# Layer norm of two quads from a host-transposed x, and a host-transposed dense weight, in a pre-norm attention layer

## The chip, the cores and the metric

The kernel runs on one core of one Trainium2 chip. The metric is the device time of one execution in microseconds (us): the median of three runs.

## What is computed

x is [8, 256, 512] float32, 2048 rows of 512. Cut to what matters, the reference is:

```
x = x + attn(layernorm(x)) ; x = x + ffn(layernorm(x))
attn: qkv = h @ w_qkv; 32 query heads, 8 key/value heads of 128; causal, bias -slope * sqrt(distance);
      out = softmax(q k^T * scale + bias) v, then out @ w_o
ffn:  dots = softmax(h @ centroids.T / 0.1); hits = dots > 0.01
      out = where(any_hit_of_row & any_hit_of_cluster[assignments], h @ weight.T + bias, 0)
```

weight is [512, 512] and centroids is [64, 512]; both are used transposed.

## The kernel before, in words

**Layout.** The 2048 rows are 4 quads of 512 (two batches each). Attention works in 32 units: unit u takes key/value head u // 4, with its 4 query heads, on quad u % 4. Float32 products go through TensorE as three passes over a high and a low part (`three_pass`), so each operand is held as `..._hi` (a copy rounded by ACT) and `..._lo` (the rest, from DVE or POOL).

**One unit on PE** is `body`: six projections (k, four q, v: `project(u, 0)` to `project(u, 5)`), with the probabilities of the unit before applied to v between them (`apply_v(u, c)`, chunks c = 0 to 5), four output projections (`project_out(u, 0)` to `(u, 3)`) and the eight score blocks `scores(u, 0)` to `(u, 7)`. Chunks 0 to 3 are applied at steps i = 2 to 5 of the projection loop, chunk 4 behind `project_out(u, 0)`, chunk 5 behind `scores(u, 1)`.

**Way of a chunk.** DVE turns 32x32 blocks of the probabilities (`turn`, L926), SP sends the tile to DRAM (`turn_out`, L399) and reads it back permuted (`turn_in`, L404), ACT makes the high part (`pT_hi_part`, L666), POOL the low part (`pT_lo_part`, L523), PE uses both. v goes the same way (`turn_v`, L418 and L430, then `v_hi_part` on ACT, L692). Every engine works in the order in which its program is written, and SP waits for each semaphore in turn: a DMA that is not ready holds back those written behind it. All of SP's DMAs go through one queue.

**Scores.** DVE adds the bias and takes the row maximum (`add_bias(u, i)`, L956 and L963), ACT takes the exponential (`exps`, L677) and scales by the reciprocal row sum (`normalise`, L686), DVE turns. `scores(u, i)` waits until `add_bias` has been done up to i - 2, since there are two banks.

**Layer norm before projection.** The norm of quad L (L = 1, 2, 3) is made inside unit L - 1, that of quad 0 ahead. DVE takes statistics (`ln_stats_of`, L847; `ln_var`, L859), ACT the root (`ln_root`, L642), DVE a refinement (`ln_scale`, L871 to L874) and the four normalised tiles (`ln_apply`, L886); PE transposes each in four 128x128 pieces (`ln_transpose`, L1270) at steps 4 and 5; ACT and DVE copy the result as `xnT` high and low (`ln_hi` L646, `ln_lo` L891). After attention the same is done for the second norm, numbered 4 to 7.

**Feed-forward weights.** In unit 29 SP loads weight, centroids, assignments and bias (L438 to L443). Ahead of unit 30 PE transposes weight and centroids in 16 + 4 pieces (L1500, L1504), ACT and DVE copy them (L795, L1153). Units 30 and 31 also carry the second norm of quads 0 and 1 and their clusters and dense products.

**Loops.** Units 0 to 2 are written out, 3 to 29 are a hardware loop on PE, ACT and DVE; SP loops over the chunks of units 0 to 28. The order of the second half of the projection loop on PE is this:

```
if lag <= i < CHUNKS - 2 + lag:
    apply_v(u, i - lag)
if L is not None and i >= 4:
    ln_transpose(L, 2 * i - 8)
    ln_transpose(L, 2 * i - 7)
```

## Time and profile before

| | |
|---|---|
| median of three runs | 1261.96 us (1261.77 to 1262.03) |
| the profiled execution's own time | 1263.28 us |
| its span, first to last instruction | 1261.6 us |
| granted TensorE clock, mean | 0.999 of full speed |
| PE busy | 1244.7 us, 99% of the span |
| DVE, ACT, POOL busy | 762.5, 752.5, 516.0 us |
| PE in the chain that ended last | 90% |

The profile is of one execution. "Unit 1" lies at about 38 to 82 us of its span, unit 2 at 82 to 120, unit 29 at 1059 to 1095, unit 30 at 1098 to 1150. Start times are counted from the first instruction. Lengths of matmuls overlap: the next one starts before the end of the last that is shown, so durations on PE are read from start to start.

### The profile page before, as it was taken

How to read it: one execution, taken by the hardware profiler on the slowest of the kernel's cores; microseconds unless marked ns; L12 is line 12 of the kernel's file. 1: busy time of each engine (PE TensorE's matmuls, PEld its weight loads, DVE VectorE, ACT ScalarE, POOL GpSimd, SP SyncE). 2: the span in 40 equal slices, each digit the busy share in tenths (PEclk: the TensorE clock that was granted, in tenths of full speed). 3: DMA queues.
4: the chain of work that ended last, by engine and by line, in shares of the span. 5: the costliest groups of instructions: out<-in, count | busy, mean ns of one | idle time of the engine just before them, and what ended most of it. 6: DMA issues, size and time to landing. Idle time of an engine off the chain costs nothing.

```text
span 1261.6 us, 21930 instructions
## 1 busy us (share of the span) xinstructions
PE 1244.7 (99%) x6188; PEld 1051.4 (83%) x6188; DVE 762.5 (60%) x2156; ACT 752.5 (60%) x2154; POOL 516.0 (41%) x476
## 2 busy tenths in 40 slices
PE   8899999999999999999999999999999999999998
PEld 7688888888888888888888888888888888888786
DVE  7777555555555555555555555655555556677677
ACT  3776555666655556666556566665566666656543
POOL 6322636227342555226442364327362364223313
PEclk9999999999999999999999999999999999999999
DMA  6422334324342344333333344323243343422103
GB/s 225 134 92 79 122 116 158 116 100 150 99 133 84 121 136 129 129 103 130 108 121 104 123 143 124 125 91 127 98 149 116 108 150 115 135 67 92 61 16 134
DMA packets 162377, 147.14 MB, mean 117 GB/s; under 512 B 10032, under 2 KB 123696, under 8 KB 162352
## 3 DMA queue, kind: packets, MB, share of 16 engines
q1 hardware_dynamic: 156528, 128.48, 30.8%
q0 software_dynamic: 5824, 18.36, 4.9%
q8 instruction: 12, 0.20, 0.1%
q14 instruction: 13, 0.11, 0.0%
HBM read 84.67 MB, written 62.13 MB: 116 GB/s over the span
## 4 chain that ended last, share of the span: by engine, by line
PE 90%; DVE 5%; ACT 2%; issue 1%; DMA 1%; POOL 0%; DVEq 0%; SPq 0%; ACTq 0%
PE ps L1250 83%; PE ps L1351 3%; PE ps L1352 1%; PE ps L1270 1%; ACT prob L677 1%; DVE stats L847 1%; ACT prob L686 1%; DVE ring_whole L926 1%; DVE qT_lo L901 1%; DVE rs L872 0%; PE ps L1280 0%; DVE prob L886 0%; DMA acc<-in_L_attn_hidden_states 0%; DVE prob L963 0%; PE ps L1382 0%
## 5 line engine op out<-in xcount | busy, mean ns | idle before, releaser
L1250 PE MATMUL ps<-xnT,wqkv_hi 128*128 (+1 forms) x1552 | 480.1, 390 | 1.3 <-DVE kT L898 1.3
L523 POOL TENSOR_TENSOR ring<-ring_whole,pT_hi 128x512 fp32r<-128x512 f32 x189 | 244.0, 1291 | 483.3 <-ACT pT_hi L666 483.0
L1250 PEld LDWEIGHTS ps<-xnT,wqkv_hi 128*128 128x128 f32 x1552 | 288.6, 188 | 61.5 <-DVE kT L898 1.7
L677 ACT ACTIVATE prob<-prob,negmax 128x128 f32<-128x128 f32 (+1 forms) x512 | 226.8, 445 | 178.3 <-DVE negmax L963 177.4
L1250 PE MATMUL ps<-xnT,wqkv_lo 128*128 (+1 forms) x776 | 302.1, 389 | 0.0
L686 ACT ACTIVATE prob<-prob,rinv 128x128 f32<-128x128 f32 (+1 forms) x512 | 190.3, 445 | 62.5 <-DVE rinv L971 62.3
L1250 PE MATMUL ps<-wo_hi,oT_hi 128*128 128x512 f32 x512 | 201.9, 394 | 0.0
L1250 PE MATMUL ps<-wo_lo,oT_hi 128*128 128x512 f32 x512 | 199.8, 390 | 0.0
L1250 PE MATMUL ps<-wo_hi,oT_lo 128*128 128x512 f32 x512 | 199.3, 389 | 0.0
L1250 PEld LDWEIGHTS ps<-xnT,wqkv_lo 128*128 128x128 f32 x776 | 145.7, 188 | 30.5
L943 DVE TENSOR_TENSOR acc<-ps,acc 128x512 f32 (+1 forms) x128 | 88.4, 691 | 127.6 <-PE ps L1250 127.4
L901 DVE SCALAR_TENSOR_TENSOR qT_lo<-ps,qT_hi 128x512 fp32r<-128x512 f32 x128 | 87.2, 681 | 118.3 <-ACT qT_hi L655 118.3
L926 DVE STREAM_TRANSPOSE ring_whole<-prob 128x512 f32<-128x512 f32 x189 | 130.0, 701 | 45.0 <-ACT prob L686 45.0
L655 ACT ACTIVATE qT_hi<-ps 128x512 fp32r<-128x512 f32 x128 | 76.2, 595 | 106.3 <-PE ps L1250 105.8
L666 ACT ACTIVATE pT_hi<-ring_whole 128x512 fp32r<-128x512 f32 x189 | 118.4, 627 | 22.7 <-DMA ring_whole<-turned 19.8
L670 ACT ACTIVATE oT_hi<-ps 128x512 fp32r<-128x512 f32 x128 | 76.0, 594 | 74.5 <-PE ps L1250 69.5
L1250 PEld LDWEIGHTS ps<-wo_hi,oT_lo 128*128 128x128 f32 x512 | 96.1, 188 | 20.4
L1250 PEld LDWEIGHTS ps<-wo_hi,oT_hi 128*128 128x128 f32 x512 | 96.3, 188 | 18.2
L1250 PEld LDWEIGHTS ps<-wo_lo,oT_hi 128*128 128x128 f32 x512 | 96.4, 188 | 17.8
L937 DVE TENSOR_TENSOR oT_lo<-ps,oT_hi 128x512 fp32r<-128x512 f32 x128 | 88.3, 690 | 32.3 <-ACT oT_hi L670 32.3
L963 DVE CUSTOM_DVE_ANT_0 prob<-ps,bias 128x256 f32<-128x256 f32 x256 | 94.3, 421 | 10.7 <-DVE ring_whole L926 8.5
L677 ACT ACTIVATION_READ_ACCUMULATOR prob<-prob,negmax 128x1 f32 x512 | 96.0, 187 | 0.0
(139 smaller groups left out, 1731.9 us busy)
## 6 DMA issues: line engine op xcount, KB each, us to landing
turned<-ring_whole SPq DMA_DIRECT2D x189, 256.0 KB, 2.1
ring_whole<-turned SPq DMA_DIRECT2D x189, 256.0 KB, 3.0
turned_v<-vT SPq DMA_DIRECT2D x32, 256.0 KB, 2.0
vT<-turned_v SPq DMA_DIRECT2D x31, 256.0 KB, 2.7
raw<-in_L_attn_w_qkv POOLq DMA_DIRECT2D x28, 256.0 KB, 3.2
raw<-in_L_attn_w_o POOLq DMA_DIRECT2D x28, 256.0 KB, 3.3
raw<-in_L_attn_w_qkv POOLq DMA_DIRECT2D x28, 128.0 KB, 3.1
acc<-in_L_attn_hidden_states SPq DMA_DIRECT2D x3, 1024.0 KB, 7.7
```

The lines of the kernel that those rows point to most:

```text
L523: pool.tensor_tensor(ring_slot(c), whole_slot(c), pT_hi[:, c % 2, :].bitcast(F32), ALU.subtract).then_inc(pT_lo_done, 1)
L655: ins = act.activation(qT_hi[:, i - 1, :], src, ACT.Copy, scale=SCALE)
L666: act.activation(pT_hi[:, c % 2, :], source, ACT.Copy).then_inc(pT_hi_done, 1)
L670: act.activation(oT_view(u, oT_hi, k), pv_view(u, k), ACT.Copy).then_inc(oT_hi_done, 1)
L677: ins = act.activation(s, s, ACT.Exp, bias=negmax[:, n:n + 1], scale=-1.0, accum_out=rowsum[:, n:n + 1])
L686: ins = act.activation(s, s, ACT.Copy, scale=rinv[:, n:n + 1])
L901: ins = dve.scalar_tensor_tensor(qT_lo[:, i - 1, :], src, SCALE, qT_hi[:, i - 1, :].bitcast(F32), ALU.mult, ALU.subtract)
L926: dve.transpose(whole_slot(c).rearrange("p (j h c) -> p h j c", h=HPG, c=BLK), source.rearrange("p h (j c) -> p h j c", c=BLK)).then_inc(p ...
L937: dve.tensor_tensor(oT_view(u, oT_lo, k), pv_view(u, k), oT_view(u, oT_hi, k).bitcast(F32), ALU.subtract).then_inc(oT_lo_done, 1)
L943: dve.tensor_tensor(acc[:, at], ps[:, out_bank(u, k), :], acc[:, at], ALU.add).then_inc(added, 1)
L963: ins = dve.tensor_tensor_reduce(out=s, in0=ps[:, score_bank(u, i), bank_col:bank_col + (qt + 1) * P], in1=bias[:, h, :] if qt else s, sca ...
L1250: ins = pe.matmul(dst, l, r, start=start and m == 0, stop=stop and m == n - 1)
```

## The change

**x by rows.** The host passes x also transposed (`in_x_t`, [512, 2048]). For quads 2 and 3, SP loads 1 MB of it (`load_xt`) straight into the place where `xnT` low of the quad will stand (`xw` is the same memory as `xnT`). DVE computes mean and scale as before, but all four statistics at step 0, and copies the means beside the scales (`ln_rows`). SP writes these 128 x 8 numbers to DRAM in token order (`send_stats`), element by element, and reads the two rows of 512 back, broadcast to all 128 partitions (`spread_stats`). POOL subtracts and multiplies chunks 0 to 2 (`centre`, `scale_xt`), DVE chunk 3 (`last_chunk`), ACT makes the high parts (`xt_hi`), POOL the low parts (`xt_lo`). The transposes, `ln_apply`, `ln_hi` and `ln_lo` of these two quads are gone. Quads 0 and 1, and the second norm, are as before.

**Dense weight and centroids.** The host passes both transposed. The 20 PE transposes are gone. The weight is loaded (1 MB) into quad 1's place of `xnT`, so SP waits until unit 29's projections are done; ACT makes the high part in unit 30 (`w_hi`, steps 2 and 3), POOL the low part between its chunks.

**Loops.** PE's unit 3 and SP's units 0 to 2 are written out.

```
+        xw = sb("xw", [P, QUADS, 2, TPQ, UT], F32, below)
-        wT_hi, wT_lo = xnT[:, 1, 0], xnT[:, 1, 1]
+        wT_hi, wT_lo, wT_raw = xnT[:, 1, 0], xnT[:, 1, 1], xw[:, 1, 1]
-        w_raw = sb("w_raw", [P, NC, HID], F32, ffn)
-        c_raw = sb("c_raw", [CLUSTERS, HID], F32, ffn)
+        c_raw = sb("c_raw", [P, NC, CLUSTERS], F32, ffn)
+        def by_rows(L):
+            return L is not None and 2 <= L < QUADS
+        def nth(L):
+            return L if L < 2 else L - 2
...
 @@ SP
+            def load_xt(L):
+                sp.dma_start(xw[:, L, 1], x_t[:, L * UT:(L + 1) * UT].rearrange("(c p) t -> p c t", p=P)).then_inc(xt_loaded, 16)
+            def send_stats(L):
+                n = L - 2
+                sp.wait_ge(stat_ready, n + 1)
+                sp.dma_start(stat_rows[n].rearrange("s (j p) -> p s j", p=P), rs[:, 4:6, :], allow_slow_non_contiguous=True).then_inc(stat_out, 16)
+            def spread_stats(L):
+                n = L - 2
+                sp.wait_ge(stat_out, 16 * (n + 1))
+                sp.dma_start(xw[:, L, 0, 2:4, :], stat_rows[n].rearrange("(a s) t -> a s t", a=1)
+                             .broadcast_to([P, 2, UT])).then_inc(stat_in, 16)
+            def turn_half_and_stats(v, L):
+                turn_out(v, 3)
+                turn_in(v, 3)
+                turn_out(v, 4)
+                send_stats(L)
+                turn_out(v, 5)
+                turn_in(v, 4)
+                spread_stats(L)
+                turn_in(v, 5)
-            with sp.Fori(0, UNITS - 3) as v:
+            turn_v(0)
+            load_xt(2)
+            turn_half(0, 0)
+            turn_half_and_stats(0, 2)
+            turn_v(1)
+            load_xt(3)
+            turn_half(1, 0)
+            turn_half_and_stats(1, 3)
+            turn_v(2)
+            turn_half(2, 0)
+            turn_half(2, 1)
+            with sp.Fori(QUADS - 1, UNITS - 3) as v:
...
-            sp.dma_start(w_raw[:], w_ffn.rearrange("(t p) d -> p t d", p=P)).then_inc(wc_loaded, 16)
-            sp.dma_start(c_raw[:], cents).then_inc(wc_loaded, 16)
+            sp.dma_start(c_raw[:], cents_t.rearrange("(c p) n -> p c n", p=P)).then_inc(c_loaded, 16)
+            sp.wait_ge(qkv_mm, PROJ_OUTS * (UNITS - QUADS + 2))
+            sp.dma_start(wT_raw, w_ffn_t.rearrange("(c p) n -> p c n", p=P)).then_inc(w_loaded, 16)
...
 @@ POOL
+            def centre(L, c):
+                if c == 0:
+                    pool.wait_ge(xt_loaded, 16 * (L - 1))
+                    pool.wait_ge(stat_in, 16 * (L - 1))
+                pool.tensor_tensor(xw[:, L, 1, c, :], xw[:, L, 1, c, :], xw[:, L, 0, 2, :], ALU.subtract).then_inc(xt_centred, 1)
+            def scale_xt(L, c):
+                pool.wait_ge(xt_centred, (NC - 1) * (L - 2) + c + 1)
+                pool.tensor_tensor(xw[:, L, 1, c, :], xw[:, L, 1, c, :], xw[:, L, 0, 3, :], ALU.mult).then_inc(xt_scaled, 1)
+            def xt_lo(L, c):
+                pool.wait_ge(xt_hi_done, NC * (L - 2) + c + 1)
+                pool.tensor_tensor(xnT[:, L, 1, c, :], xw[:, L, 1, c, :], xnT[:, L, 0, c, :].bitcast(F32),
+                                   ALU.subtract).then_inc(xt_lo_done, 1)
             for u in range(1, QUADS - 1):
-                plain_body(u)
+                for c in range(CHUNKS):
+                    pT_lo_part(u, c)
+                for c in range(NC - 1):
+                    centre(u + 1, c)
+                for c in range(NC - 1):
+                    scale_xt(u + 1, c)
+                for c in range(NC):
+                    xt_lo(u + 1, c)
+                v_lo_part(u)
...
+            u = UNITS - 2
+            for c in range(CHUNKS):
+                pT_lo_part(u, c)
+                for n in {3: (0,), 4: (1,), 5: (2, 3)}.get(c, ()):
+                    pool.wait_ge(wT_hi_done, n + 1)
+                    pool.tensor_tensor(wT_lo[:, n, :], wT_raw[:, n, :], wT_hi[:, n, :].bitcast(F32),
+                                       ALU.subtract).then_inc(wT_lo_done, 1)
+            v_lo_part(u)
...
 @@ ACT
+                    if p == 0 and i in (2, 3):
+                        w_hi(2 * i - 4)
+                        w_hi(2 * i - 3)
-                        if i == 2:
+                        if i == (1 if by_rows(L) else 2):
                             ln_root(L)
-                        if i >= 4:
+                        if i >= 4 and not by_rows(L):
...
                         elif i < 4:
+                            if by_rows(L) and i == 3:
+                                xt_hi(L, 2)
+                                xt_hi(L, 3)
                             normalise(u, i - 2)
+                            if by_rows(L) and i == 2:
+                                xt_hi(L, 0)
+                                xt_hi(L, 1)
...
 @@ DVE
+            def ln_rows(L):
+                dve.tensor_copy(rs[:, 4, :], meanvar[:, :, 0]).then_inc(stat_ready, 1)
+            def last_chunk(L):
+                dve.wait_ge(xt_loaded, 16 * (L - 1))
+                dve.wait_ge(stat_in, 16 * (L - 1))
+                x = xw[:, L, 1, NC - 1, :]
+                dve.tensor_tensor(x, x, xw[:, L, 0, 2, :], ALU.subtract).then_inc(last_centred, 1)
+                dve.wait_ge(last_centred, L - 1)
+                dve.tensor_tensor(x, x, xw[:, L, 0, 3, :], ALU.mult).then_inc(last_scaled, 1)
...
+                    if by_rows(L):
+                        if i == 0:
+                            for j in range(TPQ):
+                                ln_stats_of(L, source, j)
+                            ln_var(L)
+                        elif i == 1:
+                            ln_scale(L)
+                            ln_rows(L)
...
                 if attn:
                     add_out(u, 1)
+                if by_rows(L):
+                    last_chunk(L)
...
 @@ PE
                     if i == 0:
                         pe.wait_ge(raw_split, (u >> 2) * (2 * NC) + c + 1)
+                        if isinstance(u, int) and by_rows(u):
+                            pe.wait_ge(xt_lo_done, NC * (u - 2) + c + 1)
...
-                    if L is not None and i >= 4:
+                    if L is not None and i >= 4 and not by_rows(L):
...
-                    if L is not None and attn:
-                        pe.wait_ge(ln_lo_done, L * TPQ + TPQ)
+                    if L is not None and attn and not by_rows(L):
+                        pe.wait_ge(ln_lo_done, nth(L) * TPQ + TPQ)
...
                     pe.wait_ge(oT_lo_done, u * QTILES + QTILES)
+                    pe.wait_ge(wT_lo_done, NC)
                     dense(p, 0)
...
-            with pe.Fori(QUADS - 1, UNITS - 2) as u:
+            body(QUADS - 1, True, True)
+            with pe.Fori(QUADS, UNITS - 2) as u:
                 body(u, True, True)
-            pe.wait_ge(wc_loaded, 32)
-            pe.wait_ge(oT_lo_done, QTILES * (UNITS - 2))
-            for t in range(NC):
-                for c in range(NC):
-                    ins = pe.transpose(ps[:, WT_BANKS[t], c * P:(c + 1) * P], w_raw[:, t, c * P:(c + 1) * P], ident[:])
-                ins.then_inc(wT_mm, 1)
...
```

**SP, unit 1.** The queue of unit 1 handles the chunks of unit 0. Before (one turn of the loop, from chunk 3 on):

```order
L399 DMA turned<-ring_whole 128x512
L404 DMA ring_whole<-turned 128x4x128
L398 REGISTER_ALU
L399 DMA turned<-ring_whole 128x512
L398 REGISTER_ALU
L399 DMA turned<-ring_whole 128x512
L404 DMA ring_whole<-turned 128x4x128 x2
```

Now, from the reading back of v on:

```order
L451 DMA vT<-turned_v 128x4x128
L456 DMA xw<-in_x_t 128x4x512
L420 DMA turned<-ring_whole 128x512
L425 DMA ring_whole<-turned 128x4x128
...
L420 DMA turned<-ring_whole 128x512
L462 DMA stat_rows<-rs 128x8x1
L420 DMA turned<-ring_whole 128x512
L425 DMA ring_whole<-turned 128x4x128
L468 DMA xw<-stat_rows 128x1024
L425 DMA ring_whole<-turned 128x4x128
```

The 1 MB load stands ahead of chunk 0's way out; the statistics go out ahead of chunk 5's way out, and come back ahead of chunk 5's way in.

**DVE, unit 1,** from the turning of chunk 3. Before:

```order
L926 STREAM_TRANSPOSE ring_whole<-prob 128x4x4x32
L847 BN_STATS stats<-acc 128x6 x2
L901 SCALAR_TENSOR_TENSOR qT_lo<-ps,qT_hi 128x512
L926 STREAM_TRANSPOSE ring_whole<-prob 128x4x4x32
L847 BN_STATS stats<-acc 128x6 x2
L856 BN_AGGR meanvar<-stats 128x2 x4
L859 TENSOR_SCALAR rs<-meanvar 128x4
```

Now:

```order
L1048 STREAM_TRANSPOSE ring_whole<-prob 128x4x4x32
L956 BN_STATS stats<-acc 128x6 x4
L965 BN_AGGR meanvar<-stats 128x2 x4
L968 TENSOR_SCALAR rs<-meanvar 128x4
L1023 SCALAR_TENSOR_TENSOR qT_lo<-ps,qT_hi 128x512
L1048 STREAM_TRANSPOSE ring_whole<-prob 128x4x4x32
L980 RECIPROCAL rs<-rs 128x4
L981 TENSOR_TENSOR rs<-rs 128x4
L982 SCALAR_TENSOR_TENSOR rs<-rs 128x4
L983 SCALAR_TENSOR_TENSOR rs<-rs 128x4
L988 COPY rs<-meanvar 128x4
```

All statistics stand ahead of `proj_lo(1, 1)` and of the turning of chunk 4, and the refinement follows at once.

**SP, unit 29.** Before:

```order
L438 DMA w_raw<-in_L_ffn_weight 128x4x512
L439 DMA c_raw<-in_L_ffn_centroids 64x512
L440 DMA assigned<-in_L_ffn_assignments 64x512
L443 DMA bias_bc<-in_L_ffn_bias 128x512
L418 DMA turned_v<-vT 128x512
```

Now:

```order
L497 DMA c_raw<-in_L_ffn_centroids 128x4x64
L499 DMA xw<-in_L_ffn_weight 128x4x512
L500 DMA assigned<-in_L_ffn_assignments 64x512
L503 DMA bias_bc<-in_L_ffn_bias 128x512
L439 DMA turned_v<-vT 128x512
```

The order is nearly the same, but the weight's load waits for the sixth projection of unit 29, the one that also releases `turned_v`.

## Rows read from the trace of the kernel before

**Rows 1.** The page: busy us, share and count of each engine.

```profile
PE 1244.7 (99%) x6188; PEld 1051.4 (83%) x6188; DVE 762.5 (60%) x2156; ACT 752.5 (60%) x2154; POOL 516.0 (41%) x476
```

**Rows 2.** Timeline of PE, unit 1: start us, length us, line, operation, [idle before].

```profile
57.92 0.39 PE L1250 MATMUL ps<-pT_hi,v_lo 128*128 128x512 f32 x1
...
60.49 0.71 PE L1250 MATMUL ps<-xnT,wqkv_hi 128*128 128x512 f32 x2
...
64.02 1.04 PE L1270 MATMUL ps<-ident,prob 128*128 128x128 f32 x8
64.81 0.48 PE L1250 MATMUL ps<-wo_hi,oT_hi 128*128 128x512 f32 x1
...
69.18 0.45 PE L1250 MATMUL ps<-pT_hi,v_hi 128*128 128x512 f32 x1
...
77.24 0.34 PE L1351 MATMUL ps<-kT,qT_hi 128*128 128x256 f32 x1
```

**Rows 3.** Timeline of PE, unit 2.

```profile
97.60 0.60 PE L1270 MATMUL ps<-ident,prob 128*128 128x128 f32 x4
...
98.91 0.71 PE L1250 MATMUL ps<-xnT,wqkv_hi 128*128 128x512 f32 x2
```

**Rows 4.** Timeline of PE, end of unit 29, the weight's turn, unit 30.

```profile
1094.73 0.40 PE L1250 MATMUL ps<-kT,qT_hi 128*128 128x256 f32 x2
...
1095.45 1.91 PE L1500 MATMUL ps<-ident,w_raw 128*128 128x128 f32 x16
...
1097.99 0.73 PE L1250 MATMUL ps<-xnT,wqkv_hi 128*128 128x512 f32 x2
```

**Rows 5.** Timeline of SP's DMA issues, chunks of unit 0 (during unit 1).

```profile
36.97 0.37 SPq L430 DMA_DIRECT2D vT<-turned_v  x1
40.11 0.33 SPq L399 DMA_DIRECT2D turned<-ring_whole  x1
42.12 0.37 SPq L404 DMA_DIRECT2D ring_whole<-turned  x1
...
57.58 2.13 SPq L404 DMA_DIRECT2D ring_whole<-turned  x2
```

**Rows 6.** Timeline of SP's DMA issues, the feed-forward loads in unit 29.

```profile
1073.92 0.37 SPq L438 DMA_DIRECT2D w_raw<-in_L_ffn_weight  x1
...
1078.70 0.34 SPq L418 DMA_DIRECT2D turned_v<-vT  x1
1084.60 0.38 SPq L430 DMA_DIRECT2D vT<-turned_v  x1
```

**Rows 7.** DMA issues on the page (count, KB each, us to landing), and L385's landings.

```profile
ring_whole<-turned SPq DMA_DIRECT2D x189, 256.0 KB, 3.0
...
vT<-turned_v SPq DMA_DIRECT2D x1, 128.0 KB, 2.3
...
DMA to landing us min/median/max: 5.3/7.7/9.9
```

**Rows 8.** Timeline of ACT, units 1 and 29.

```profile
46.16 0.51 ACT L677 ACTIVATE prob<-prob,negmax 128x256 f32<-128x256 f32 x1 [0.31 <-DVE negmax L963]
...
1087.42 0.63 ACT L692 ACTIVATE v_hi<-vT 128x512 fp32r<-128x512 f32 x1 [1.69 <-DMA vT<-turned_v]
```

**Rows 9.** Timelines of DVE and POOL near 14 us, and the page's L523.

```profile
13.98 1.72 DVE L1133 TENSOR_TENSOR wqkv_lo<-acc,wqkv_hi 128x768 fp32r<-128x768 f32 x1
14.83 2.57 POOL L480 TENSOR_TENSOR wqkv_lo<-acc,wqkv_hi 128x768 fp32r<-128x768 f32 x1
L523 POOL TENSOR_TENSOR ring<-ring_whole,pT_hi 128x512 fp32r<-128x512 f32 x189 | 244.0, 1291 | 483.3 <-ACT pT_hi L666 483.0
```

**Rows 10.** Timeline of DVE, units 1, 29 and 30.

```profile
75.13 0.17 DVE L971 RECIPROCAL rinv<-rowsum 128x4 f32<-128x4 f32 x1
...
1094.04 0.29 DVE L963 CUSTOM_DVE_ANT_0 prob<-ps,prob 128x128 f32<-128x128 f32 x1
...
1114.08 0.99 DVE L886 TENSOR_SCALAR prob<-acc,meanvar,rs 128x512 f32<-128x512 f32 x2
```

More of the change, by code:

```diff
@@ L42, with build @@
 QTILES = 4
-def build(nc, x_in, w_qkv, w_o, w_ffn, b_ffn, cents, assign, out):
+def build(nc, x_in, x_t, w_qkv, w_o, w_ffn_t, b_ffn, cents_t, assign, out):
     ctx = ExitStack()
@@ L68, in build @@
         query_sel = sb("query_sel", [P, 2, TPQ], F32)
+        below = ExitStack()
+        xw = sb("xw", [P, QUADS, 2, TPQ, UT], F32, below)
+        below.close()
         att = ExitStack()
@@ L122, in build @@
         ffn.close()
+        stat_rows = [nc.dram_tensor(f"stat_rows{n}", [2, UT], F32, kind="Internal").ap() for n in range(2)]
         turned = nc.dram_tensor("turned", [CHUNKS, P, 512], F32, kind="Internal").ap()
@@ L188, in build @@
         ln_lo_done = sem("ln_lo_done")
+        xt_loaded = sem("xt_loaded")
+        stat_ready = sem("stat_ready")
+        stat_out = sem("stat_out")
+        stat_in = sem("stat_in")
+        xt_centred = sem("xt_centred")
+        xt_scaled = sem("xt_scaled")
+        last_centred = sem("last_centred")
+        last_scaled = sem("last_scaled")
+        xt_hi_done = sem("xt_hi_done")
+        xt_lo_done = sem("xt_lo_done")
         ffn_step = sem("ffn_step")
@@ L644, in ln_hi, with xt_hi @@
             def ln_hi(L, j, quad):
-                act.wait_ge(ln_mm, L * TPQ + j + 1)
+                act.wait_ge(ln_mm, nth(L) * TPQ + j + 1)
                 act.activation(ln_part(quad, 0, j), ps[:, ln_bank(L, j), :].rearrange("p (c t) -> p c t", c=NC),
                                ACT.Copy).then_inc(ln_hi_done, 1)
+            def xt_hi(L, c):
+                act.wait_ge(xt_scaled, (NC - 1) * (L - 2) + (c + 1 if c < 2 else NC - 1))
+                if c >= 2:
+                    act.wait_ge(last_scaled, L - 1)
+                act.activation(xnT[:, L, 0, c, :], xw[:, L, 1, c, :], ACT.Copy).then_inc(xt_hi_done, 1)
             def proj_hi(u, i):
@@ L725, in scaled_bias, with w_hi @@
                                    scale=selects(p)[:, j:j + 1]).then_inc(bias_scaled, 1)
+            def w_hi(c):
+                act.wait_ge(w_loaded, 16)
+                act.activation(wT_hi[:, c, :], wT_raw[:, c, :], ACT.Copy).then_inc(wT_hi_done, 1)
             def body(u, proj, attn, L=None, quad=None, p=None, lag=2):
@@ L881, in ln_apply @@
                     dve.wait_ge(p_turned, u * CHUNKS)
-                if not (isinstance(L, int) and L == 0):
-                    dve.wait_ge(ln_mm, L * TPQ - TPQ + j + 1)
-                    if j >= PROB_TILES and not (isinstance(L, int) and L >= 6):
-                        dve.wait_ge(ln_mm, L * TPQ + 1)
+                if L > 0:
+                    dve.wait_ge(ln_mm, nth(L) * TPQ - TPQ + j + 1)
+                    if j >= PROB_TILES and L < 6:
+                        dve.wait_ge(ln_mm, nth(L) * TPQ + 1)
                 dve.tensor_scalar(ln_tile(L, j), acc[:, rows(quad, j, 1)], meanvar[:, j, 0:1], rs[:, 5, j:j + 1],
```

60 lines of the change are left out of this document (26 added, 34 removed).

## The prediction

> **What bounds the kernel now.** I read the page first, for which engine fills the span: PE is busy 99% of it, DVE and ACT 60%, POOL 41% [rows 1]. So a change pays only by what it takes off PE's program or out of its waits, and costs whatever makes PE wait. Next came PE's timeline in the places that the change touches, where the reader should see from start to start how long the transposes hold PE [rows 2 to 4]; then SP's list of DMA issues there, for the order in the one queue and for the time at which the next issue shows the last landing [rows 5, 6], and the landing times [rows 7]; then ACT and DVE, for how much later each could have been without PE noticing [rows 8, 10]; last a place where DVE and POOL both work in SBUF [rows 9].
>
> **What goes off PE.** Unit 1: after the matmul at 57.92 the next would start one step, 0.23, later, at 58.15; the projection resumes at 60.49, so the first two groups of transposes hold PE 2.3 us, half of it waiting for DVE. The other two take 64.02 to 64.81, 0.8 [rows 2]. Unit 2: 97.60 to 98.91 is 1.3 [rows 3], and its second pair is the same work as unit 1's, 0.8. Weight and centroids: 1095.45 to 1097.99, 2.5 [rows 4]. Together 32 + 20 transposes, **7.7 us**, and there is no cover over them: it is all on the path.
>
> **What comes back.** Five things, each a wait that is not there before.
>
> *The load of x in unit 1.* SP issues it behind the reading back of v at 36.97, so at 37.4, and 2.7 us later chunk 0 goes out behind it, at 40.11, where it landed by 42.12 [rows 5]. The queue keeps its order: `turned_v`, issued at 1078.70 behind the 1.5 MB begun at 1073.92, landed at 1084.60, after 5.9 us instead of 2.0 [rows 6]. A load of 1 MB landed after 5.3 us at best, 7.7 in the middle [rows 7]; with the end of v ahead of it I take 6, so 43.4, and chunk 0 about 0.4 behind it, 43.8, which is 1.7 late. ACT takes chunk 0 in without idling, and idles 0.31 right behind it [rows 8]; ACT's exponentials and the k copy behind them are what PE waits for in unit 1. So 1.7 - 0.3 = **1.4** is lost. The ends: 0, if the engines serve both, and 3.2 with 7.7 for the load. In unit 2 the load is issued some 11 us before chunk 0, and costs nothing.
>
> *The statistics in the queue.* They are ready in unit 1 at about 56 to 57, as DVE does them in one go. No row shows a DMA of 1024 packets of 4 bytes. The nearest are 512 packets in 2.3 and 3.0 [rows 7], against 2.0 for 128 packets [rows 5]; 1024 make about 4, between 2.0 and 6. Then 512 KB are spread, and chunk 5's way in, issued at 59.3 before (the second of the two at 57.58 [rows 5]), goes out at about 60.9 behind them. It lands 3.0 [rows 7] plus some 1.7 for the 512 KB later, at 65.6; ACT adds 0.6 [rows 8], POOL 1.3 [rows 9]: 67.5. PE wants it at 69.18 [rows 2] less the 3.1 taken off in unit 1, plus the 1.4 that delay all engines alike, which cancel: 66.1 against 67.5. Since SP, POOL and ACT can start some of it sooner than my latest times, I take half, **0.7** (0 to 3). In unit 2 only 2.1 have gone off PE by then, so there is 1 us more room: 0.
>
> *The two operations on DVE* (`last_chunk`), one in each of units 1 and 2, fall into POOL's run of `centre` and `scale_xt`. Rows 9 show what that means: DVE's operation on 768 columns starts at 13.98 and ends at 15.70, 1.72 for what would need some 0.9 alone (1.5 x 0.6 for 512 columns, my estimate from the 0.5 of a tile with one input [rows 10]); POOL's, shown from 14.83, takes 2.57 where 768 columns need 1.5 x 1.29 = 1.94. They take turns in SBUF, whole instructions each. So DVE's two need 1.2 alone and up to 3.8; I take 2.9, half a POOL instruction ahead of the first and nearly a whole one ahead of the second. The cover: the bias of score block 3 was done at 75.13 [rows 10], and block 5, which waits for it, started at 77.24 [rows 2], 2.1 later. That leaves 0.8. Behind it ACT has `xt_hi`, four copies of about half a us [rows 8] between its exponentials, and the probabilities of half a unit pass it later; I add 0.3. Twice 1.1 is **2.2** (0 to 4).
>
> *The weight's load in unit 29.* It may start only after the sixth projection, at about 1077.9, 4.0 us later than before, at the very moment at which v is to go out. With assignments and bias it needs 7 to 8 us, so v is out at about 1087 instead of 1084.60 [rows 6]. ACT waited 1.69 for it already at 1087.42 [rows 8], so all of 2.4 delays ACT. Block 7 of the scores, at 1094.73 [rows 4], waits for a bias done at 1094.33 [rows 10]: 0.4 of cover, and I allow 1.0 for DVE's wait for PE between. It leaves **1.0** (0 to 2.5).
>
> *Unit 30.* POOL's four `wT_lo` of 1.29 stand between its chunks. DVE's `ln_apply`, at 1114.08, needs 0.5 for each tile [rows 10] and is of the kind that takes turns with POOL. PE is already waiting for it there, as in unit 2. **0.8** (0 to 1.3).
>
> At nothing I cost: the copies taken from ACT and DVE (60% busy, waiting for others at that place); ACT's `w_hi`, under a wait for PE in unit 30; the ten instructions of 1.29 on POOL per quad, 12.9 us, which follow chunk 5 at about 67 and end near 81, just before unit 2's projections at about 82 minus the gain want them (`v_lo(1)` is queued behind, and is wanted 5 us into unit 2). If that cover is gone, PE waits at `xt_lo_done`, up to 2 us. The loop's unrolling costs nothing: units 1 and 2 were written out already.
>
> **The sum.** 7.7 - 1.4 - 0.7 - 2.2 - 1.0 - 0.8 = 1.6 us gained. The profiled execution took 1263.28 in all, so 1261.7 for the changed kernel; the median shown lies 1.3 lower, at 1261.96, and so the forecast is 1260.4. A measurement of this kernel tells 0.2%, 2.5 us, from no change.
>
> **A page against the row.** Writing 1024 single elements to DRAM is what the row of 2.3 us [rows 7] bounds only from afar. The Trainium skill's "VectorE: DVE Perf Modes", section "The three transpose paths", says that a plain DMA with transposing strides is 19 times slower than the X-bar's 1309 ns for 128x128. By it 1024 elements would need an estimated 1.6 us over the fixed time, 3.6 in all where I take 4, and the sum would be 0.2 to 0.4 better; nothing here shows it.
>
> **Rivals.** *Most of it stays.* The five waits lie under slack that I count too small: DVE's two operations slip between POOL's (1.2 in place of 2.9, covered by the 2.1), chunk 5 is in time, DVE and POOL miss each other in unit 30. For it: ACT and DVE get four to eight instructions fewer just there. Against: rows 9. What is left is the load of x, 1.4, and half of the weight's, 0.5, with some 0.8 of small waits: 7.7 - 2.7 = 5.0, so 1257.0.
>
> *The small packets are slow, and it is slower than before.* If the statistics land after 8 us rather than 4, chunk 5 comes 4 later. PE waits 4.0 more in unit 1 and 3.0 in unit 2, where 1 us was left: 1.6 - 7.0 = -5.4, so 1267.4. It decides from about 6.2 us of landing on, where the gain becomes a loss of 2.5. For it: every chunk behind shares the queue. Against: halving the run from 512 to 256 bytes, at the same number of packets, made the landing shorter, 2.3 for 3.0 [rows 7]. The Trainium skill's "DMA: Bandwidth & Descriptors", section "Specifications", speaks for it: below 512 bytes the DMA does read-modify-write. No run here shows that for writes to DRAM.
>
> **How the numbers follow.** The forecast gets 0.52, most staying 0.36, slow packets 0.12. The forecast's own range is about 1258.5 to 1263.5; of its 0.52 I give 0.03 to faster by over 0.2% and 0.01 to slower. That makes faster 0.39, same 0.48, slower 0.13. The range for 8 in 10 reaches from 1256.0, just beyond the second case, to 1264.2, where the terms of unit 1 are at their upper ends, and leaves out the slow packets.
>
> **What would show it.** Right: 52 fewer matmuls on PE; in unit 1 ACT's first copy of a chunk waits for its DMA some 1.5 us; a wait of PE of about 0.7 ahead of chunk 5; waits of PE for DVE ahead of score blocks 4 to 7 in units 1 and 2, about 1 us each; DVE's `last_chunk` instructions over 1 us long; ACT waiting some 4 us for v in unit 29. From first projection to first projection, the sum says: unit 1 as long as before (3.1 - 1.4 - 0.7 - 1.1 = -0.1), unit 2 1.0 shorter (2.1 - 1.1), units 29 and 30 with the weight 0.7 shorter (2.5 - 1.0 - 0.8). Wrong: a landing of the statistics above 6 us; or blocks 4 to 7 without a wait, which would give the second rival.

## The result and the profile after

The changed kernel takes **1281.62 us** (median of 4 runs, 1280.77 to 1282.54), the kernel before 1261.87: the ratio is 1.0155, 95% interval 1.0143 to 1.0167, so 20 us slower. The prediction said 1260.4, within 1256.0 to 1264.2. It was wrong. The profiled execution took 1282.54, its span is 1280.9.

| from first projection to first projection, us | unit 1 | unit 2 | units 3 to 29 | from unit 30 on |
|---|---|---|---|---|
| before | 43.44 | 38.43 | 977.64 | 163.6 |
| after | 55.51 | 48.14 | 975.01 | 163.8 |
| difference | +12.07 | +9.71 | -2.63 | +0.2 |

The loss lies in units 1 and 2 alone. Everything else together gained 2.5. (The +0.2 from unit 30 on flatters the change: in the profiled execution of the kernel before, the granted clock of TensorE, PE's engine, was 0.50 for some 3 us near the end, and 18 matmuls that take 4.3 in the other runs took 6.0 there.) PE issues 52 matmuls fewer, is busy 2.6 longer all the same, and its share falls from 99% to 97% (page, against [rows 1]; below it that stretch of the kernel before: busy time of PE, PEld, DVE, ACT, POOL, then granted clock, DMA share, GB/s):

```profile
PE 1247.3 (97%) x6136; PEld 1051.7 (82%) x6136; DVE 756.2 (59%) x2142; ACT 751.7 (59%) x2154; POOL 545.5 (43%) x500
```

```profile
1236.00:1237.00 1.00, 1.00 (x3) 0.73 (x3) 0.85 (x3) 0.00 (x0) 0.00 (x0) 0.50 0.00 0
```

SP's list of DMA issues in unit 1, to be read against [rows 5] (start, length of the issue, line):

```profile
40.05 0.33 SPq L420 DMA_DIRECT2D turned<-ring_whole  x1
44.32 0.36 SPq L425 DMA_DIRECT2D ring_whole<-turned  x1
...
59.02 0.36 SPq L462 DMA_DIRECT2D stat_rows<-rs  x1
...
61.21 0.43 SPq L425 DMA_DIRECT2D ring_whole<-turned  x1
70.48 0.33 SPq L468 DMA_DIRECT2D xw<-stat_rows  x1
70.86 0.44 SPq L425 DMA_DIRECT2D ring_whole<-turned  x1
```

Chunk 0 is read back (L425) at 44.32 for 42.12 before, 2.2 late where the prediction had 1.7. The largest new thing is at 59.02: the statistics go out, and the issue that waits for them comes at 70.48, **11.4 later** where the prediction had about 4. The DMA issues' list (last number: median landing), and the landings of L425:

```profile
stat_rows<-rs SPq DMA_DIRECT2D x2, 4.0 KB, 11.2
```

```profile
DMA to landing us min/median/max: 2.7/3.0/10.0
```

Chunk 4, whose reading back is issued at 61.21 right behind, is caught in it as well: L425's longest landing is 10.0 for a median of 3.0. ACT shows both chunks arriving, and PE pays (timelines of ACT and PE; in brackets the idle time before and who ended it; the last row is unit 2):

```profile
71.27 0.63 ACT L767 ACTIVATE pT_hi<-ring_whole 128x512 fp32r<-128x512 f32 x1 [10.35 <-DMA ring_whole<-turned]
...
76.06 0.63 ACT L767 ACTIVATE pT_hi<-ring_whole 128x512 fp32r<-128x512 f32 x1 [3.67 <-DMA ring_whole<-turned]
...
49.66 0.50 PE L1377 MATMUL ps<-pT_hi,v_hi 128*128 128x512 f32 x1 [2.89 <-POOL ring L583]
...
51.49 1.17 PE L1377 MATMUL ps<-xnT,wqkv_hi 128*128 128x512 f32 x2 [0.86 <-DVE kT L1020]
...
73.30 0.79 PE L1377 MATMUL ps<-pT_hi,v_hi 128*128 128x512 f32 x1 [6.89 <-POOL ring L583]
...
78.09 0.79 PE L1377 MATMUL ps<-pT_hi,v_hi 128*128 128x512 f32 x1 [1.55 <-POOL ring L583]
...
122.02 0.79 PE L1377 MATMUL ps<-pT_hi,v_hi 128*128 128x512 f32 x1 [6.14 <-POOL ring L583]
```

What else happens there stands in the stretches (busy time of PE, PEld, DVE, ACT, POOL, then granted clock, DMA share, GB/s):

```profile
50.00:55.00 5.00, 4.14 (x11) 2.94 (x10) 3.84 (x7) 4.98 (x14) 0.44 (x1) 0.66 0.41 135
60.00:65.00 5.00, 5.00 (x24) 4.14 (x23) 3.29 (x6) 0.84 (x2) 0.23 (x1) 1.00 0.92 42
65.00:70.00 5.00, 1.40 (x7) 0.82 (x5) 0.00 (x0) 0.00 (x0) 0.00 (x0) 0.86 1.02 52
70.00:75.00 5.00, 1.70 (x5) 1.42 (x6) 1.29 (x2) 1.11 (x2) 1.26 (x1) 0.50 0.54 173
75.00:80.00 5.00, 3.45 (x13) 2.88 (x13) 1.78 (x10) 3.02 (x7) 3.23 (x3) 0.50 0.53 180
```

From 60 to 70 the DMA engines count as full (0.92, 1.02) and move 42 to 52 GB/s, less than a third of the 173 to 180 in 70 to 80. And TensorE's clock, 2.4 GHz, was granted at half, 1.2 GHz, from 70 to 80 (by the finer stretches, from 69 to 82), after PE had idled. The same is seen smaller at 50 to 55 (0.66), behind the wait of 2.89 for chunk 0.

**Where the time of a unit goes.** PE's timeline gives five stretches in each unit, from start to start of the same matmuls: A, from the first projection to `project_out(u, 0)`; B, on to chunk 4's product; C, on to chunk 5's; D, on to `scores(u, 2)`; E, on to the next unit's first projection. The stretches are those of the profiled execution, the medians those of all executions of the run. Against the kernel before (unit 1: 26.33, 2.82, 1.55, 3.47, 9.27; unit 2: 21.32, then the same):

| kernel, unit | A | B | C | D | E | sum | median, us |
|---|---|---|---|---|---|---|---|
| after, 1 | -1.23 | +6.96 | +3.24 | +2.02 | +1.08 | +12.07 | 1281.62 |
| after, 2 | -2.25 | +6.20 | +2.69 | +1.85 | +1.22 | +9.71 | |
| stats_act_queue, 1 | -1.25 | +8.58 | +1.50 | +0.36 | +1.95 | +11.14 | 1281.73 |
| busy_wait, 1 | -1.37 | +8.27 | +2.33 | +2.56 | +0.55 | +12.34 | 1281.19 |
| busy_long, 1 | -1.42 | +7.83 | +3.59 | +1.67 | +1.15 | +12.82 | 1283.81 |
| own_rows, 1 | -1.26 | +1.53 | +3.30 | +2.70 | +0.39 | +6.66 | 1271.55 |
| stats_turned, 1 | -1.30 | +0.25 | +2.26 | +0.07 | +1.52 | +2.80 | 1265.45 |
| stats_turned, 2 | -2.26 | -0.10 | +1.74 | +0.05 | +1.54 | +0.97 | |
| load_early, 1 | -2.82 | +0.21 | +2.07 | +1.69 | +1.10 | +2.25 | 1263.76 |
| in5_first, 1 | -3.24 | +0.09 | +0.24 | +0.10 | +1.49 | -1.32 | 1258.92 |
| in5_first, 2 | -2.27 | -0.10 | +0.01 | 0.00 | +1.33 | -1.03 | |
| last_later, 1 | -2.93 | +0.13 | +0.12 | 0.00 | +3.41 | +0.73 | 1263.15 |
| all_pool, 1 | -3.03 | +0.25 | +0.12 | +0.03 | 0.00 | -2.63 | 1256.97 |
| all_pool, 2 | -1.79 | +0.51 | +0.12 | +0.03 | 0.00 | -1.13 | |

Read downwards: B and C are the late chunks, D the low clock behind chunk 5, E what DVE does between the scores, A the gain of the transposes less the wait for chunk 0. The other rows are the experiments below.

### The profile page after: what moved, and what is told of

Same layout as the page of the kernel before. It is cut to its first block, busy times and chain, and to the rows that moved or that the text cites. A ratio compares the mean times of both kernels' runs of the same rounds, so it can differ in the third digit from the quotient of the medians.

```text
span 1280.9 us, 21780 instructions
## 1 busy us (share of the span) xinstructions
PE 1247.3 (97%) x6136; PEld 1051.7 (82%) x6136; DVE 756.2 (59%) x2142; ACT 751.7 (59%) x2154; POOL 545.5 (43%) x500
## 4 chain that ended last, share of the span: by engine, by line
PE 84%; DVE 6%; ACT 3%; DMA 3%; issue 2%; POOL 1%; SPq 0%; DVEq 0%; ACTq 0%; POOLq 0%
PE ps L1377 79%; PE ps L1480 3%; DMA ring_whole<-turned 2%; ACT prob L778 1%; ACT prob L787 1%; PE ps L1481 1%; DVE stats L956 1%; DVE ring_whole L1048 1%; PE ps L1397 1%; DVE qT_lo L1023 1%; DMA turned_v<-vT 0%; DVE prob L1085 0%; POOL ring L583 0%; PE ps L1407 0%; DMA turned<-ring_whole 0%
## 5 line engine op out<-in xcount | busy, mean ns | idle before, releaser
L1377 PE MATMUL ps<-kT,qT_hi 128*128 128x256 f32 x512 | 95.4, 284 | 1.4 <-DVE negmax L1085 1.0
```

What stands on the lines that cost most here:

```text
L1377: ins = pe.matmul(dst, l, r, start=start and m == 0, stop=stop and m == n - 1)
```

## The experiments

Theory A: the 1024 packets of 4 bytes are what is slow, they delay whatever else the DMA moves meanwhile, and PE's wait lets its clock fall. Its rival: the place in the queue and the 512 KB spread.

**stats_turned.** The statistics are turned in SBUF first, so that they leave as 4 x 8 rows of 128 bytes.

```diff
-  dve.tensor_copy(rs[:, 4, :], meanvar[:, :, 0]).then_inc(stat_ready, 1)
+  dve.tensor_copy(rs[:, 4, :], meanvar[:, :, 0]).then_inc(stat_copied, 1)
+  dve.wait_ge(stat_copied, L - 1)
+  dve.transpose(xw[:, L, 0, 0, 0:BLK], rs[:].rearrange("p a t -> p (a t)")).then_inc(stat_ready, 1)
...
-  sp.dma_start(stat_rows[n].rearrange("s (j p) -> p s j", p=P), rs[:, 4:6, :], ...)
+  for b in range(P // BLK):
+      sp.dma_start(stat_rows[n].rearrange("s (j b c) -> b (s j) c", b=P // BLK, c=BLK)[b],
+                   xw[b * BLK + 4 * TPQ:b * BLK + 6 * TPQ, L, 0, 0, 0:BLK]).then_inc(stat_out, 16)
```

> Edit: the statistics are turned by one DVE transpose of 32x32 blocks first and go out in four DMAs of 8 packets of 128 bytes each, in place of one DMA of 1024 packets of 4 bytes; all else as in the changed kernel. Theory A (the 1024 packets of 4 bytes hold the 16 DMA engines for 11 us, the chunks behind them arrive 8 us late, and PE's long idle time lowers its clock): the landing falls to about 2, the waits of 6.9 and 1.6 and the half clock disappear from units 1 and 2, and the time falls by 20 or more, to 1257 to 1261. Theory B (the queue: 512 KB spread and the two extra issues ahead of chunk 5 are what delays it, whatever the packets are): the time stays above 1275.

1265.45 (ratio 1.0021, 1.0012 to 1.0030): 16 of the 20 us are gone, and stretch B with them. So the way in which the statistics go out is the cause of B. Number, length and layout of the packets changed together here; price_list and own_rows part them. It missed 1257 to 1261: PE still waits for chunk 5, whose way in stands behind the 512 KB (C, 2.26 and 1.74; in5_first moves it), and E is 1.5 in each unit:

```profile
69.30 0.50 PE L1385 MATMUL ps<-pT_hi,v_hi 128*128 128x512 f32 x1 [1.98 <-POOL ring L587]
```

**weight_only.** Only the weight and centroids come from the host; `by_rows` returns False, and SP, POOL and PE have their old code for quads 2 and 3.

> Edit: only the weight and the centroids are laid out by the host; quads 2 and 3 are normalised and transposed as before. By the trace of the changed kernel (units 3 to 29 took 2.6 less, from unit 30 on 0.2 more): 2.4 below before, 1259.5. By the prediction's terms (2.5 - 1.0 - 0.8): 0.7 below, 1261.2.

1260.59 (ratio 0.9983, 0.9974 to 0.9992), 1.8 below the 1262.42 of the kernel before beside it, with an interval from 1.0 to 3.3. The units say 975.25 and 163.95, so 2.4 and -0.3. This half of the change pays, by more than the forecast 0.7. (The loss of 0.3 is too small by up to 1.6, for the low clock of the kernel before that the section on the result shows.)

**busy_wait and busy_long.** Ahead of the wait for chunk 4:

```diff
                     project_out(u, 0)
+                    if L is not None and by_rows(L):
+                        pe.wait_ge(oT_lo_done, u * QTILES + 2)
+                        for _ in range(40):       # 72 in busy_long
+                            pe.transpose(ps[:, PV[1], 0:P], ident[:], ident[:])
                     apply_v(u, CHUNKS - 2)
```

> Edit: ahead of the wait for chunk 4 in units 1 and 2, PE does 40 transposes of the identity (about 4.8 us at the 0.12 of a transpose) into the bank that the next product overwrites. Theory A (part of the loss is the clock that falls during PE's idle time, and halves PE's speed for the 7 us of work behind): the granted clock stays at 1.00 or falls later, and 3.5 us come back in each of the two units, so 1274 to 1275, although nothing arrives earlier. Rival (the waits alone cost it, the low clock only covers time that PE would have waited anyway for chunk 5): 1281 to 1282, as before this edit.

> Edit: as busy_wait with 72 in place of 40 transposes (8.6 us). There 3.8 us of PE's wait were left, and the clock fell all the same at its end. Theory (the clock's part of the loss is real, and comes back once the wait is filled): granted clock 1.00 through units 1 and 2 up to the wait for chunk 5, and 3 to 3.5 us back in each, 1274 to 1276. Rival: 1281.

1281.19 and 1283.81: nothing back. In busy_wait the clock fell at the end of the 3.83 that were left. In busy_long it stayed at 1.00 through the wait:

```profile
68.00:70.00 2.00, 2.00 (x21) 2.00 (x20) 0.00 (x0) 0.00 (x0) 0.00 (x0) 1.00 0.72 99
...
80.00:82.00 2.00, 2.00 (x6) 1.52 (x6) 0.04 (x1) 0.60 (x2) 2.00 (x3) 0.50 0.65 251
```

```profile
77.72 0.49 PE L1377 MATMUL ps<-pT_hi,v_hi 128*128 128x512 f32 x1 [3.31 <-POOL ring L583]
```

PE was only faster at reaching the next wait, 3.31 for chunk 5, whose time is set by the DMA, and behind it the clock fell after all (0.50 at 80 to 82). So theory A was wrong in this part: the low clock ahead of chunk 5 was covered by waiting. What it costs is stretch D, 1.7 to 2.0 in each unit, where PE works at half speed on its critical path, and that part busy_long did not remove.

**price_list.** Single DMAs, SBUF to DRAM, on quiet queues, behind the last store of the kernel before; each is waited for, so the time to the next issue is its whole price.

> Edit: the kernel before, and behind its last store, with nothing else on the queues, single DMAs from SBUF to DRAM one after the other, each waited for: 1024, 512 and 256 packets of 4 bytes in the layout of the statistics; then 1024 packets of 4, 32, 128 and 512 bytes with a row for each partition; 128 packets of 32 bytes; four times 8 packets of 128 bytes. Theory A (each packet costs the same, about 0.15 us on one of 16 engines, small or not): about 11, 6.5 and 4 us for the first three, and 1024 packets of 32 or 128 bytes take as long as of 4. Theory B (what costs is that a packet is far below 512 bytes): 1024 packets of 4 bytes take 11, those of 512 bytes clearly less. Theory C (the layout: neighbours of 4 bytes in one row of DRAM come from different partitions): 1024 packets of 4 bytes with a row for each partition land in 4 to 5. Four times 8 packets: about 2 each.

```profile
1258.85 0.38 SPq L463 DMA_DIRECT2D columns_out<-acc  x1
1267.57 0.38 SPq L463 DMA_DIRECT2D columns_out<-acc  x1
1277.45 0.36 SPq L463 DMA_DIRECT2D columns_out<-acc  x1
1286.50 0.36 SPq L463 DMA_DIRECT2D pieces_out<-acc  x1
1291.22 0.36 SPq L463 DMA_DIRECT2D pieces_out<-acc  x1
1293.38 0.36 SPq L463 DMA_DIRECT2D pieces_out<-acc  x1
```

```profile
1260.00:1261.00 1.00, 0.00 (x0) 0.00 (x0) 0.00 (x0) 0.00 (x0) 0.00 (x0) 0.50 0.31 3
...
1264.00:1265.00 1.00, 0.00 (x0) 0.00 (x0) 0.00 (x0) 0.00 (x0) 0.00 (x0) 0.50 0.00 0
```

In order: 1024, 512 and 256 packets of 4 bytes side by side by partition take **8.7, 9.9 and 9.1**, with no trace of the count. 1024 packets of 4 bytes in places 32 bytes apart: 4.7. Of 32 bytes: 2.2, of 128: 2.2, of 512 (512 KB): 3.6. And 8 packets of 128 bytes: 1.2. Theory A's price for each packet falls, as does B: far below 512 bytes is not slow in itself. C, the layout, stands. The stretches of the first DMA show no traffic after 1261, and for the other 6 us nothing moves that the trace records.

**price_list2.** The same with other layouts.

> Edit: the kernel before, and behind its last store single DMAs from SBUF to DRAM, each waited for, with nothing else on the queues. In this order: 128, 32 and 16 elements of 4 bytes side by side from as many partitions; 128 elements 32, 64 and 512 bytes apart; 1024 elements 64 and 256 bytes apart, eight of each partition; 1024 elements of 8 bytes side by side by partition; 128 packets of 32 bytes side by side. Theory N64 (writes into the same 64 bytes follow one another, about 0.5 each, 16 of them making the 9): about 9, 9, 9; 2, 1.3, 1.3; under 2.5, under 2.5; 5; 1.5. Theory N512 (the same, with 512 bytes): about 9, 3, 2; 2, 1.7, 1.3; 4, 2.5; 6 or more; 1.5.

```profile
1260.61 0.33 SPq L463 DMA_DIRECT2D pieces_out<-acc  x1
1268.09 0.34 SPq L463 DMA_DIRECT2D pieces_out<-acc  x1
1273.01 0.32 SPq L463 DMA_DIRECT2D pieces_out<-acc  x1
1275.48 0.34 SPq L463 DMA_DIRECT2D pieces_out<-acc  x1
1276.90 0.34 SPq L463 DMA_DIRECT2D pieces_out<-acc  x1
```

128, 32 and 16 elements side by side, each from another partition: 7.5, 4.9, 2.5. 128 of them 32, 64 or 512 bytes apart: 1.4 each time. 1024 at 64 and 256 bytes apart: 3.6 and 2.8. Elements of 8 bytes side by side (512 of them; the expectation says 1024): 4.4, half of the price. So it is closeness that costs: sixteen elements side by side, 64 bytes in all, take 2.5, while 128 of them with sixteen in each 512 bytes take 1.4. Both laws fall as stated: N64 wanted 9 for the sixteen, N512 wanted 2 for the 128 at 32 bytes, and neither gives 7.5 and 4.9. The exact law stays open.

**stats_act_queue.** The same 4-byte DMA on ACT's queue (`act.dma_start` behind ACT's fifth copy of the projections), chunk 5 read back ahead of the spreading.

> Edit on the changed kernel: the same DMA of 1024 packets of 4 bytes is issued by ACT on ACT's queue (behind its fifth copy of the projections), the rest stays on SP's; chunk 5 is read back ahead of the spreading. Theory Q (the slow small writes hold up only what is behind them on their own queue; the engines are free, as the price list shows, where most of the 9 us passes with no traffic): chunks 4 and 5 arrive 3 us after their issue, PE's waits of 6.9 and 6.1 and the half clock behind them go, and the time falls by some 20, to 1258 to 1263. Theory E (the small packets hold the 16 engines themselves): chunk 4 is late whatever the queue, and the time stays above 1275.

1281.73 (ratio 1.0160): no gain, theory Q falls. SP's and ACT's issues and ACT's wait (timeline; the statistics landed 12.4 after their issue, median of the two):

```profile
57.24 4.06 SPq L420 DMA_DIRECT2D turned<-ring_whole  x2
61.34 11.57 SPq L425 DMA_DIRECT2D ring_whole<-turned  x2
...
59.75 0.40 ACTq L825 DMA_DIRECT2D stat_rows<-rs  x1
...
73.00 0.63 ACT L760 ACTIVATE pT_hi<-ring_whole 128x512 fp32r<-128x512 f32 x1 [11.97 <-DMA ring_whole<-turned]
```

Chunk 4, issued on SP's queue at 61.34, still lands more than 11 after its issue, where 3.0 is the median. What blocks is behind the queues and shared by these two. Whether it is the 16 engines or the memory isn't told apart by these runs.

**own_rows.** The 1024 packets 32 bytes apart, in a scratch of their own (`stat_own`, eight places for each partition); two rows of x are spread instead, so quads 2 and 3 are normalised with other numbers.

> Edit on the changed kernel: the 1024 packets of 4 bytes go to places 32 bytes apart, each partition's eight next to each other, in a scratch of their own, instead of side by side with those of other partitions; what is spread is two rows of x in place of the statistics, so quads 2 and 3 are normalised with wrong numbers at the same cost. Theory N (small writes of different partitions into the same stretch of DRAM wait for each other; in the first price list 256, 512 and 1024 of them took 8.7 to 9.9, and 1024 of them in rows of their own 4.7): the landing falls from 11 to 5 or 6, PE's wait for chunk 4 from 6.9 to about 1, and the time to 1268 to 1272. Theory P (the number of packets under 512 bytes decides): landing 11, time 1281.

1271.55 (ratio 1.0079, 1.0065 to 1.0093), landing 5.4: half of the loss gone with as many packets as before. Stretch B falls to 1.5. This is in the kernel what the price list shows beside it.

**load_early.** On top of stats_turned, `load_xt(2)` goes behind `load_x(3)` at the start.

> Edit on top of stats_turned: the load of x for quad 2 is issued behind the last load of x at the start, not behind v in unit 1. Theory (the 1 MB ahead of chunk 0 cost 2.0 of waiting in unit 1 and let the clock fall to half for 3.5 us behind it): in unit 1 the first product with v moves from offset 11.1 back to 8.8, no half clock, so about 3.5 less, 1262. Rival (PE's waits in unit 1 come from ACT's chain of exponentials, the load only covers them, or the load takes its time from the start instead): no change, 1265.

1263.76 (ratio 1.0019), whose interval overlaps that of stats_turned, so the time alone doesn't show it. Stretch A does: -2.82 for -1.30, so the load cost unit 1 **1.5**. In this profiled execution the clock fell behind PE's wait of 1.79 for chunk 5 (stretch D, +1.69), which hid the gain; in that of stats_turned it stayed at 1.00 behind one of 1.98 (D, +0.07). The two together show what the low clock costs in D, and that the wait's length alone doesn't decide whether it falls.

**in5_first.** On top of it, `turn_in(v, 5)` goes ahead of `spread_stats(L)`.

> Edit on top of load_early: chunk 5 is read back ahead of the spreading of the statistics. Theory (the 512 KB ahead of chunk 5 make the 1.7 that PE waits for it in each of units 1 and 2): 3 less than load_early. Rival (the statistics then come later, POOL ends later, and the next unit's first projection waits): no gain or up to 1 of it.

**1258.92** (ratio 0.9976, 0.9967 to 0.9986), 4.8 below load_early: more than the 3 expected, since with the wait for chunk 5 (C, +2.07 to +0.24) the low clock behind it goes too (D, in unit 1). What is left is stretch E. DVE and POOL there, and the low parts of unit 30 (timelines):

```profile
70.89 1.13 DVE L1003 TENSOR_TENSOR xw<-xw 128x512 f32<-128x512 f32 x1
72.05 1.66 DVE L1005 TENSOR_TENSOR xw<-xw 128x512 f32<-128x512 f32 x1
...
70.17 4.69 POOL L674 TENSOR_TENSOR xw<-xw 128x512 f32<-128x512 f32 x3
...
1107.39 1.27 DVE L988 SCALAR_TENSOR_TENSOR rs<-rs 128x4 f32<-128x4 f32 x1
1108.70 1.46 DVE L1016 TENSOR_SCALAR prob<-acc,meanvar,rs 128x512 f32<-128x512 f32 x1
...
1108.60 1.27 POOL L705 TENSOR_TENSOR xnT<-xw,xnT 128x512 fp32r<-128x512 f32 x1
```

DVE's two (L1003, L1005) take 1.13 and 1.66, and POOL's three take 4.69 for 3.8: the turns that [rows 9] showed.

**last_later.** On top of in5_first, `last_chunk(L)` goes behind `add_out(u, 2)`.

> Edit on top of in5_first: DVE's two operations on the last chunk of x go behind add_out(u, 2), where DVE was idle for 1.0 and POOL had ended its scaling, not behind add_out(u, 1), where they took 1.13 and 1.66 beside POOL's. Theory (they and their wait for POOL cost 1.3 in each of units 1 and 2): each back to 0.6, unit 2 from 37.4 to 36.5 or less, the time 1.5 to 2 lower, 1257. Rival (the 1.3 come from ACT's four copies of x between its exponentials): no change, 1259.

1263.15 (ratio 1.0009, 1.0000 to 1.0019), 4 worse. I had put DVE's two where it was idle, but without them before it ACT's copies and POOL's low parts came sooner (73.58 for 77.30), and POOL was now at work there:

```profile
75.46 1.67 DVE L1005 TENSOR_TENSOR xw<-xw 128x512 f32<-128x512 f32 x1
...
77.22 1.15 ACT L752 ACTIVATE xnT<-xw 128x512 fp32r<-128x512 f32 x2 [2.21 <-DVE xw L1005]
...
78.97 0.51 PE L1385 MATMUL ps<-kT,qT_hi 128*128 128x256 f32 x2 [2.12 <-DVE negmax L1093]
```

They take 1.59 and 1.67, ACT waits 2.2 for them with its exponentials behind, and PE 2.1.

**weight_slots.** On top of last_later, POOL's slots for `wT_lo` become `{2: (0,), 4: (1,), 5: (2, 3)}`.

> Edit on top of last_later: POOL makes the first low part of the weight behind chunk 2 instead of chunk 3, where it ran from 1108.6 beside DVE's 1.27 for four elements and 1.46 for one tile. Theory (DVE and POOL take turns in SBUF, and that delays the first transposes of unit 30 by 1.2): PE's waits there shrink, 0.7 to 1.2 less than last_later. Rival (DVE is late there for other reasons): no change.

1261.56, 1.6 below last_later. From unit 30 on it took 162.7 for 163.6, so 0.9 of that are the slot's: the wait of 0.95 ahead of the first transposes is gone, that of 0.34 behind it stays.

**all_pool and all_pool_slots.** On top of in5_first, POOL centres and scales all NC chunks, DVE none; then the slots of weight_slots as well.

```diff
-  for c in range(NC - 1):
+  for c in range(NC):
       centre(u + 1, c)
-  for c in range(NC - 1):
+  for c in range(NC):
       scale_xt(u + 1, c)
...
-  if by_rows(L):
-      last_chunk(L)
```

> Edit on top of in5_first: POOL centres and scales all four chunks of x, DVE none; POOL was idle there for 2.4 before its low parts, and two more operations need 2.6. Theory D (DVE's two operations, 1.1 to 1.7 each beside POOL's, make the 1.3 by which unit 2 is longer than a unit of the loop): unit 2 from 37.4 to 36.1 to 36.4, unit 1 as much shorter, the time 2 to 2.5 lower, 1256.5 to 1257. Theory A (ACT's four copies between its exponentials make it): unit 2 stays at 37.4, or grows where POOL ends later, 1259 or more.

> Edit on top of all_pool: POOL's first low part of the weight behind chunk 2 in place of chunk 3, as in weight_slots, where it took 1.6 off last_later. If that holds here: 1.2 to 1.6 below all_pool, 1255 to 1256 by theory D, 1257.5 by theory A, and 5 to 7 below the kernel before by D. Rival: without DVE's late start the slot no longer collides, and nothing changes.

```profile
66.09 5.06 POOL L669 TENSOR_TENSOR xw<-xw 128x512 f32<-128x512 f32 x4
71.10 5.06 POOL L674 TENSOR_TENSOR xw<-xw 128x512 f32<-128x512 f32 x4
76.11 5.07 POOL L679 TENSOR_TENSOR xnT<-xw,xnT 128x512 fp32r<-128x512 f32 x4
```

1256.97 (ratio 0.9961, 0.9948 to 0.9975): POOL's chain has no gap now, each operation takes its 1.27, and stretch E is back to 9.27 in both units, with ACT's four copies still in place. So theory D holds for E. Unit 2 itself missed its 36.1 to 36.4: it came down to 37.30 only, since A and B are longer by 0.5 and 0.6 than in in5_first (in all_pool_slots by 0.5 and 0.8). PE waits there at 81.33 for POOL's last low part of x, 0.22, and later 0.45 for chunk 4: POOL's longer chain takes back part of the gain. With the slots **1256.36** (ratio 0.9953, 0.9939 to 0.9966), 5.6 below the 1262.0 of the kernel before beside it, and the best of all. The 0.6 between the two is within their scatter; PE's wait of 0.95 in unit 30 is gone in the second.

## Why the prediction was wrong, step by step

**What goes off PE (7.7).** Right. In in5_first stretch A is 3.24 and 2.27 shorter (3.1 and 2.1 forecast), and units 3 to 29 are 2.59 shorter for the 2.5 of [rows 4]. The best version, all_pool_slots, keeps 5.6 of it.

**The statistics in the queue (0.7). This is the step that failed**: "1024 make about 4, between 2.0 and 6". I scaled the landing with the number of packets, from rows whose packets are 256 and 512 bytes long, and which read DRAM where this DMA writes it [rows 7]. It was 11.0 and 11.4. On quiet queues the count hardly matters (256 take as long as 1024), and the layout does. The upper bound was not a bound: no row of the kernel before writes single elements side by side from different partitions, and I had no reason to stop at 6. Second, I counted only what is queued behind the DMA, chunk 5; chunk 4 was issued 2.2 after it and was 7 late, and another queue does not help. Third, the clock: no term spoke of it, and it cost some 2 in each unit.

The same term was too small in its other half too. With the slow packets gone (stats_turned), chunk 5 still cost 2.26 and 1.74 in stretch C, where I had 0.7 and 0, and 1265.45 would still have lain above the range. Its way in was issued 24.7 after the unit's start, where my figures say 22.4. I had no term for DVE's new order: with all four statistics ahead of chunk 4, DVE turned chunk 5 at 21.9 of unit 1, for 18.0 before, and still at 19.9 with the load of x out of the way (in5_first). There the cover holds it (C, +0.24); with 512 KB ahead of it, it does not.

**The rival.** *The small packets are slow* had the mechanism and the sign, 8 us of landing and 1267.4. With the 11.2 measured, its own working (chunk 5 late by 7 rather than 4) gives 3.2 more for each unit, 1273.8. The other 8 are not in its working: chunk 4's delay, the low clock and DVE's order. (Its own threshold is off too: by its terms the gain becomes a loss of 2.5 at 6.6 us of landing, not at 6.2.) It stood outside the range with a chance of 0.12, which "8 in 10" allowed and the evidence did not: a price that no row shows should not have been given 4 and an end of 6. What spoke against it, that 512 packets of half the length landed sooner, was about another layout.

**The two pages of the Trainium skill.** By the Trainium skill's "VectorE: DVE Perf Modes", section "The three transpose paths", I worked out 3.6 for the landing, near my 4. The traces say 11.2, and 8.7 alone. The Trainium skill's "DMA: Bandwidth & Descriptors", section "Specifications", has read-modify-write below 512 bytes, and spoke for the rival. The price list shows no jump of the landing there: 1024 packets of 32 and of 128 bytes, none beside another, land in 2.2, those of 512 bytes, with 4 to 16 times as much data, in 3.6. On the rate, which that line of the page is about, it says little. That elements of 4 bytes in the same 64 are slow and the same elements 64 bytes apart are not would fit writes that read first and wait for each other, but that is a guess: no run shows a read.

**The load of x (1.4).** Right: 1.5 by stretch A. Not foreseen was that the clock falls for 3 us behind the wait of 2.89 (0.66 at 50 to 55).

**The two operations on DVE (1.1 in each unit).** Right: 1.1 and 1.2 in stretch E of the changed kernel, 1.3 to 1.5 where POOL's run lies fully beside them. Together they took 2.79 where I had 2.9.

**The weight's load in unit 29 (1.0).** Too dear. ACT waited 2.90 for v (1.69 before), so v was 1.2 later and not 2.4, and PE shows no wait: units 3 to 29 are 2.63 shorter, all that was hoped for.

```profile
1110.26 0.63 ACT L793 ACTIVATE v_hi<-vT 128x512 fp32r<-128x512 f32 x1 [2.90 <-DMA vT<-turned_v]
...
1134.00 0.63 PE L1397 MATMUL ps<-ident,prob 128*128 128x128 f32 x4 [1.09 <-DVE prob L1008]
1134.96 0.66 PE L1397 MATMUL ps<-ident,prob 128*128 128x128 f32 x4 [0.33 <-DVE prob L1008]
```

**Unit 30 (0.8).** Right in place and mechanism, 1.2 in size: in in5_first DVE's L1016 takes 1.46 for one tile (0.55 before), beside POOL's `wT_lo` at 1108.60. (L988's 1.27 for four elements of each partition lie beside POOL's low part of a chunk; such rows are in the kernel before too.) In the kernel before PE waited 0.31 there, now 1.09 and 0.33.

**Without the failed step.** in5_first has neither the slow landing nor the load of x nor the 512 KB ahead of chunk 5. Its sum is 7.7 less the 2.8 of DVE's two operations less the 1.2 of unit 30, so 3.7; measured were 3.3. So the account closes there. The terms other than the statistics were sound or too dear, and together smaller than the one that I had sized from the wrong rows.
